# Shared expert moved into the routed expert loop, bodies of 18 tiles, gates applied as rows leave PSUM

## The reference, cut to what matters

```python
x = x + tanh(g_xattn) * xattn(layernorm(x), ctx_768)      # 16 heads, 77 keys
flat = layernorm(x)                                       # 8192 tokens x 128
scores = softmax(flat @ router_w.T + router_bias)         # 32 experts
topk_scores, topk_idx = top_k(scores, 4)                  # normalised to sum 1
h = silu(flat @ gate_w[e].T) * (flat @ up_w[e].T)         # per chosen expert e, H = 128
out = sum_k topk_scores[k] * (h @ down_w[e_k].T)
out = out + silu(flat @ sgate_w.T) * (flat @ sup_w.T) @ sdown_w.T   # shared expert, 512 wide
x = x + tanh(g_ffn) * out
```

## Time and profile before

| | |
|---|---|
| runs | 1175.61, 1176.28, 1176.44 us, median 1176.28 |
| profiled execution | span 1462.0 us; no other time of it is given |
| attention and routing, to about 760 us of the trace | 760 us |
| table and two shared chunks, 760 to 804 us | 44 us |
| expert loop, 804 to 1304 us | 500 us |
| tail, 1304 to 1462 us | 158 us |
| busy over the span | PE 79%, DVE 54%, ACT 51%, POOL 46% |

### The profile page before, as it was taken

How to read it: one execution, slowest core, us unless ns; L and a number is a source line. 1 busy time by engine, 2 the same in 40 slices (tenths; PEclk the granted TensorE clock), 3 DMA queues, 4 the chain that set the end, 5 groups by cost and what they waited for, 6 DMA issues and landing times.

```text
span 1462.0 us, 27745 instructions
## 1 busy us (share of the span) xinstructions
PE 1161.1 (79%) x6592; PEld 874.1 (60%) x6593; DVE 784.3 (54%) x3017; ACT 746.2 (51%) x2533; POOL 673.6 (46%) x947
## 2 busy tenths in 40 slices
PE   5888988888888888888876776676767766779997
PEld 3666766666766766666753555454555555545664
DVE  4766666666665666666652333333333333338777
ACT  4776766776766776766741433343333333322221
POOL 1355555454545454555563555555555555540000
PEclk9988889898898989989978888888878788889999
DMA  6200000000000000001212222222222222225443
GB/s 179 92 25 24 26 28 27 24 24 24 28 25 27 25 24 24 24 28 29 102 41 70 76 79 72 77 77 71 72 70 74 74 73 76 70 65 154 133 120 109
DMA packets 90282, 89.96 MB, mean 62 GB/s; under 512 B 21293, under 2 KB 71578, under 8 KB 89876
## 3 DMA queue, kind: packets, MB, share of 16 engines
q1 hardware_dynamic: 72468, 55.17, 13.7%
q0 software_dynamic: 17792, 34.53, 7.0%
HBM read 49.57 MB, written 42.16 MB: 63 GB/s over the span
## 4 chain that ended last, share of the span: by engine, by line
PE 55%; issue 13%; another core or an unknown queue 12%; ACT 12%; DVE 4%; DMA 2%; POOL 1%; ACTq 0%; SPq 0%; POOLq 0%; DVEq 0%
PE ps L1067 9%; PE ps L976 7%; PE ps L1032 6%; PE ps L936 6%; ACT qT L510 5%; PE ps L1078 4%; PE ps L1041 3%; PE ps L1073 3%; PE ps L941 2%; PE ps L1062 2%; PE ps L1015 2%; PE ps L1018 2%; PE ps L913 2%; ACT sg L571 1%
## 5 line engine op out<-in xcount | busy, mean ns | idle before, releaser
L432 POOL DMA_INDIRECT y_rows<-y_sb,didx x288 | 283.0, 983 | 236.0 <-DVE y_sb L839 140.7
L414 POOL DMA_INDIRECT x_rows<-payload,slot x256 | 251.3, 982 | 220.9 <-DVE slot L754 158.5
L1067 PE MATMUL ps<-w_gu,xT 128*128 x576 | 211.4, 454 | 70.4 <-issue 68.6
L571 ACT ACTIVATE sg<-ps 128x128 f32<-128x128 f32 x288 | 80.9, 281 | 269.4 <-PE ps L1067 120.1
L828 DVE TENSOR_TENSOR h<-sg,ps 128x128 f32<-128x128 f32 x288 | 82.9, 288 | 206.2 <-ACT sg L571 113.6
L976 PE MATMUL ps<-kvbd,qT 128*128 128x308 f32 x512 | 191.4, 484 | 0.0
L936 PE MATMUL ps<-vt,pT 128*128 128x108 f32 x1024 | 162.4, 309 | 0.0
L936 PEld LDWEIGHTS ps<-vt,pT 128*128 128x128 f32 x1024 | 145.0, 219 | 14.1 <-issue 9.2
L1067 PEld LDWEIGHTS ps<-w_gu,xT 128*128 128x128 f32 x576 | 105.3, 228 | 79.7 <-issue 79.5
L1073 PE MATMUL ps<-cst,h 128*128 128x128 f32 x288 | 96.9, 337 | 68.2 <-issue 38.6
L839 DVE COPY y_sb<-ps 128x128 f32<-128x128 f32 x288 | 82.7, 287 | 120.9 <-remote 81.6
(11 more groups left out here) (130 smaller groups left out, 2288.2 us busy)
## 6 DMA issues: line engine op xcount, KB each, us to landing
xin<-x_rows SPq DMA_DIRECT2D x288, 64.5 KB
w_gu<-y_rows SPq DMA_DIRECT2D x16, 1024.0 KB, 5.7
y_rows<-y_sb,didx POOLq DMA_INDIRECT x288
w_gu<-in_gu SPq DMA_DIRECT2D x2, 2048.0 KB, 10.1
x_rows<-payload,slot POOLq DMA_INDIRECT x256
out<-w_gu SPq DMA_DIRECT2D x16, 256.0 KB, 2.5
w_dn<-in_dn SPq DMA_DIRECT2D x1, 2048.0 KB, 9.2
ctx_sb<-in_ctxT SPq DMA_DIRECT2D x64, 29.2 KB
```

Source lines behind the costliest of these rows:

```text
L414: nc.gpsimd.indirect_dma_start(x_rows, bass.IndirectOffsetOnAxis(ap=slot[:, v, k:k + 1], axis=0), payload[:, v, k, :], None).then_inc(sent ...
L432: nc.gpsimd.indirect_dma_start(y_rows, bass.IndirectOffsetOnAxis(ap=didx[:, u:u + 1], axis=0), y_sb[:, u, :], None, bounds_check=TOKENS * ...
L1067: nc.tensor.matmul(bank[2 + u % 2][:, 0:2 * H], xT[:, u % 2, :], w_gu[:, bass.ds(e * (2 * H), 2 * H)], start=True, stop=True).then_inc(gu_ ...
```

## The change

1. The expert loop runs 16 bodies of `U3` = 18 tiles. `xin` and `y_sb` have 18 slots each. At the head of a body PE reads 20 numbers and SP 18.
2. The first 12 bodies (`MID`) each hold one chunk of the shared expert, a unit from each of the tiles 0, 4, 9 and 13 (`UNIT_AT`): its gate matmul in that tile, its up matmul one tile later, its product on DVE two later, its down matmuls three later. The tail keeps chunks 14 and 15.
3. The shared expert needs three PSUM banks in the loop, so three of the four results of a tile have one bank (`ps_xT`, `ps_hT`, `ps_dn`). `turn_x` now waits for the copy of the turn before, `down` for the copy of the result before (`y_d`), and PE's order within a tile is `gate_up`, `down`, `turn_h`, `turn_x`.
4. A row of `x_rows` carries its gate as a 130th column. `result` multiplies by it where it only copied. `take_dest` and `didx` are gone: POOL takes the row numbers from `xin`, so a slot of `xin` is free only when its scatter has landed.
5. The tail sums in place: four additions of 512 columns a chunk on `x_all`, from four slots of loaded rows; the stores read `x_all`.

```diff
-U3 = 8
+U3 = 18
+PER = 2
+UNIT_AT = (0, 4, 9, 13)
+MID = 12
...
+        ps_xT, ps_gu, ps_hT, ps_dn, ps_g, ps_u, ps_y = bank[0], bank[1:3], bank[3], bank[4], bank[5], bank[6], bank[7]
...
+        def bodies(eng, body):
+
+            body(0, shared=True, first=True)
+            with eng.Fori(1, MID) as j:
+                body(j, shared=True)
+            with eng.Fori(MID, TG - 1) as j:
+                body(j, shared=False)
+            body(TG - 1, shared=False, last=True)
...
                 for u in range(U3):
 
-                    tile_done(sp, didx_d, n, u)
+                    need(sp, y_sent[u], 16 * j)
                     sp.dma_start(xin[:, u, :], x_rows[bass.ds(firsts[u], 128), :]).then_inc(xin_in[u], 16)
...
-                nc.vector.tensor_copy(didx[:, u:u + 1], xin[:, u, D:ROW].bitcast(U32)).then_inc(didx_d[u % 4], 1)
...
-                nc.vector.tensor_copy(y_sb[:, u % U3, :], bank[6 + u % 2][:, 0:D]).then_inc(y_d[u % 4], 1)
+                nc.vector.tensor_scalar(y_sb[:, u % U3, :], ps_dn[:, 0:D], xin[:, u % U3, D + 1:ROW], None,
+                                        ALU.mult).then_inc(y_d[u % PER], 1)
...
+            def body(j, shared, first=False, last=False):
+                n = counts(dve, j, U3 // PER)
                 for u in range(U3):
                     hidden(n, u)
                     if not (first and u < 2):
                         result(n, u - 2)
+                    if shared and u - 2 in UNIT_AT:
+                        mixed_hidden(j, UNIT_AT.index(u - 2))
+                if shared:
+                    mixed_take(j)
...
+                for k in range(TOPK):
+                    if k:
+                        dve.wait_ge(acc_d, TOPK * c + k)
+                    nc.vector.tensor_tensor(xs, xs, yld[:, c % 4, :, k, :], ALU.add).then_inc(acc_d, 1)
...
                 for u in range(U3):
                     gate_up(n, u, es[u + 2])
+                    if shared and u in UNIT_AT:
+                        mixed_gate(j, UNIT_AT.index(u))
+                    if shared and u - 1 in UNIT_AT:
+                        mixed_up(j, UNIT_AT.index(u - 1))
+                    if shared and u - 3 in UNIT_AT:
+                        mixed_down(j, UNIT_AT.index(u - 3))
+                    if not (first and u < 2):
+                        down(n, u - 2, es[u])
                     if not (first and u == 0):
                         turn_h(n, u - 1)
                     if not (last and u >= U3 - 2):
-                        turn_x(n16, u + 2)
-                    if not (first and u < 2):
-                        down(n, u - 2, es[u])
+                        turn_x(n16, n, u + 2)
```

More of the change, by code:

```diff
@@ L36 @@
 EARLY = 2
-ROW = D + 1
+MID = 12
+ROW = D + 2
 STRIDE = TOKENS + 128
@@ L90, in build @@
         x2T = sb("x2T", [128, T])
-        gates = sb("gates", [128, B * TOPK])
         tg = sb("tg", [128, 2])
@@ L585, in body @@
                         evac(n, u + 2)
+                    if shared and u in UNIT_AT:
+                        mixed_silu(j, UNIT_AT.index(u))
             for u in range(2):
                 evac(counts(act, 0, 1), u)
[L589 to L596, removed]
+            bodies(act, body)
+            h_turned(counts(act, TG - 1, U3 // PER), U3 - 1)
+            with act.Fori(EARLY + MID, CHUNKS) as j:
                 for u in range(4):
@@ L843, in body, with mixed_take @@
+            def mixed_take(j):
+                c = EARLY + j
+                xs = x_all[:, bass.ds(c * 4 * D, 4 * D)]
+                need(dve, sy_p, 16 * c + 16)
+                nc.vector.scalar_tensor_tensor(out=xs, in0=ps_y[:, :], scalar=tg[:, 1:2], in1=xs,
+                                               op0=ALU.mult, op1=ALU.add).then_inc(take_d, 4)
+            def body(j, shared, first=False, last=False):
+                n = counts(dve, j, U3 // PER)
                 for u in range(U3):
@@ L886, in _ @@
-            with dve.Fori(1, CHUNKS // 2 - 1) as j:
-                chunk(2 * j + 1, 1)
-                chunk(2 * j + 2, 0)
-            chunk(CHUNKS - 1, 1)
+                combine(c - late)
             take(CHUNKS - 1)
-            for k in range(TOPK):
-                combine(CHUNKS - 1, 1, k)
+            for c in range(CHUNKS - late, CHUNKS):
+                combine(c)
         @block.tensor
@@ L1081, in tiles, with units, mixed_gate @@
-            def tiles(j, first=False, last=False):
+                tile_done(pe, y_d, n, u - 1)
+                after(nc.tensor.matmul(ps_dn[:, 0:D], hT[:, u % 2, :], w_dn[:, bass.ds(e * D, D)], start=True,
+                                       stop=True), hT_d, n, u).then_inc(dn_p[u % PER], 1)
+            def units(j, k):
+                unit = 4 * (EARLY + j) + k
+                return unit if isinstance(unit, int) else pe.to_reg(unit)
+            def mixed_gate(j, k):
+                unit = units(j, k)
+                nc.tensor.matmul(ps_g[:, :], w[:, W_SG + 128 * k:W_SG + 128 * (k + 1)],
+                                 x2T_all[:, bass.ds((EARLY + j) * 512, 512)], start=True,
+                                 stop=True)._wait_ge(ssg_d, unit).then_inc(sg_p, 1)
@@ new lines, in mixed_up, with mixed_down @@
+            def mixed_up(j, k):
+                unit = units(j, k)
+                nc.tensor.matmul(ps_u[:, :], w[:, W_SU + 128 * k:W_SU + 128 * (k + 1)],
+                                 x2T_all[:, bass.ds((EARLY + j) * 512, 512)], start=True,
+                                 stop=True)._wait_ge(hs_d, unit).then_inc(sg_p, 1)
+            def mixed_down(j, k):
+                unit = 4 * (EARLY + j) + k
+                need(pe, hs_d, unit + 1)
+                if k == 0:
+                    need(pe, take_d, unit)
+                for q in range(4):
+                    nc.tensor.matmul(ps_y[:, q * D:(q + 1) * D], hs[:, k % 2, q * 128:(q + 1) * 128],
+                                     w[:, W_SD + 128 * k:W_SD + 128 * (k + 1)], start=k == 0 and q == 0,
+                                     stop=k == NS - 1 and q == 3).then_inc(sy_p, 1)
@@ L1083, in tiles, with body @@
+            def body(j, shared, first=False, last=False):
                 es = numbers(pe, tab_sb, j * TW + U3, U3 + 2, E - 1)
-                n, n16 = counts(pe, j, U3 // 4), counts(pe, j, 2, dma=True)
+                n, n16 = counts(pe, j, U3 // PER + 1), counts(pe, j, 2, dma=True)
                 for u in range(U3):
                     gate_up(n, u, es[u + 2])
+                    if shared and u in UNIT_AT:
+                        mixed_gate(j, UNIT_AT.index(u))
[5 more added lines that the diff above has]
+                        down(n, u - 2, es[u])
```

181 lines of the change are left out of this document (81 added, 100 removed).

## The result

The changed kernel takes 1244.96 us (median of 4 runs, 1244.07 to 1246.05), the one before 1176.13 us beside it: a ratio of 1.058, interval 1.057 to 1.060. The forecast was +17 us; the runs gave +69. Its sign holds, its size does not.

The account below looks back on a forecast made before the run. POOL was taken to bound the old loop and plain bodies, PE the bodies with a chunk. Tail -74, loop +90 and tables +1 gave +17 us, 1193 us against 1176, with a range of 1132 to 1218.

Parts of the forecast that it names:

- The budget of before: Time of the kernel before by stage: tail 158 us, 64 attention steps 552, start, drain and table about 70, loop 388.
- unexplained stretches: Pieces in the loop and attention of the first profile that no instruction explains, such as 3.41 us, read as profiling cost.
- POOL as the bound of the old loop: A scatter every 1.29 us on POOL against 0.87 us a tile on PE; PE idles 0.42 us a tile.
- The tail: Tail after the change, with 8 units and 16 chunks of sums: 78 to 95 us, taken as 84, saving 74 us.
- Wait one: In bodies with a chunk, `mixed_down` in tile u+3 waits 0.79 us for `hs` from DVE, 3.2 us in four units.
- Wait two: With one PSUM bank, `down` waits for the previous tile's `result`: mostly covered beside chunks, plain tiles 0.87 to about 1.05 us.
- Wait three, the boundary: PE's pause between bodies, with 20 numbers to load: bounded by 1.6 and 3.1 us, taken as 2.1 us.
- The falling clock: Rival, chance 0.12: first two tiles behind each boundary at half clock, 1.7 us lost twelve times, +20 us, 1213 us.
- the 31.4 us forecast: Length of a loop body with a chunk: 26.1 us of PE work, 3.2 for `hs`, 2.1 for the boundary; twelve times 377.

Follow-up runs that it names:

- aligned run: Changed kernel with table rows padded to 160 bytes, so that both groups of numbers start on a multiple of 16 bytes: 1214.61 us, ratio 1.033.
- the one with every body off: Changed kernel with rows of 160 bytes but PE's numbers 8 bytes past a multiple of 16 in every body: 1272.37 us, ratio 1.085.
- eight chunks spread: Changed kernel, table aligned, last projection one tile later, two units in each of 16 bodies at tiles 4 and 13: 1133.6 us, ratio 0.967.

## Why the forecast was wrong in size

**The budget of before** (tail 158, loop 388, unexplained stretches not real) was right within 5 us, and POOL as the bound of the old loop too.

**The tail** took 70 us, forecast 84. The additions were as bounded, 0.69 us each:

```profile
L895 DVE TENSOR_TENSOR x_all<-x_all,w_gu x64: 680/692/694, 1182.2 to 1240.7; 128x512 f32<-128x512 f32 x64
```

What was off is the rate: 300 GB/s at a share of 0.86, where the earlier trace rows had 253 at 0.81. The Trainium skill's 425 GB/s for a large load ("DMA: Bandwidth & Descriptors", Bandwidth) would have put it, by an estimate, at some 65 us. Over the whole tail this case shows 300, nearer the row than the page, and the time of 70 us lies nearer the estimate's.

**Wait one** (0.79 us at `hs`) was right: 0.70 us in the rows above, and in the run with the projection a tile later it is gone.

**Wait two** was right for plain tiles: PE's own time for a plain body with a short load is 21.8 us in the aligned runs, forecast 21. In bodies with a chunk I counted it as covered by shared matmuls "in most tiles", and put the others at nothing. With the projection a tile later, 29.35 us less 1.5 for the pause leave 27.9 us where 26.1 were forecast. The trace of the aligned kernel with the later projection shows where they are, in two following tiles without a shared matmul:

```profile
846.54 0.60 PE L1084 MATMUL ps<-w_gu,xT 128*128 x2
847.55 0.60 PE L1084 MATMUL ps<-w_gu,xT 128*128 x2
847.64 0.27 ACT L592 COPY hT<-ps 128x128 f32<-128x128 f32 x1 [0.19 <-PE ps L1089]
847.68 0.34 DVE L856 TENSOR_SCALAR y_sb<-ps,xin 128x128 f32<-128x128 f32 x1
848.17 0.48 PE L1095 MATMUL ps<-w_dn,hT 128*128 x2
848.71 0.60 PE L1084 MATMUL ps<-w_gu,xT 128*128 x2
```

The tiles take 1.01 and 1.16 us from start to start, and those with a shared matmul 0.87 and the matmul (1.73 us). In the second tile `down` (L1095) could start 0.43 us behind `gate_up`, at 847.98. It starts 0.15 us behind the end of `y_sb` at 848.02, the copy out of its one result bank; `hT` had ended at 847.91. In the first tile the two end within 0.02 us of each other. That is wait two. Eight of the 18 tiles are such tiles: 4 x (1.01 + 1.16 - 2 x 0.87) = 1.7 of the 1.8 us. A second result buffer was not tried; by these rows it would not remove all of it, since `hT` comes only a little earlier.

**Wait three, the boundary, is the step that failed.** "I bound the boundary by 1.6 (length does not matter) and 3.1 us (twice) and take 2.1." I took min 1.07 and median 1.84 of the earlier trace rows as a spread around one price. They are two prices, by the start address, and the one boundary of the earlier trace rows was a short one. With 20 numbers the long price is 4.9 us, the pause 5.8. The aligned run puts this at 30 us, the one with every body off at another 27.

**The falling clock**, a rival at 0.12 and +20 us, held beside it, and the sum had it at nothing. I had argued that a pause of 1.57 us stood at clock 1.00. That row covers the pause alone, but the body behind it had no half clock either, and such pauses keep the clock in all profiles but that stretched first one. Those of the changed kernel are 2.3 and 5.8 us. The Trainium skill ("TensorE: Matmul & The Clock Gate", HAM oscillation) tells of a loop that waits some 3 to 5 us for a transfer in each pass and starts each pass cold. The forecast stretched that to its own pause of 2 us, which the page does not state. Here every body with a chunk of the changed kernel had half clock, behind 2.0 to 5.8 us, and none behind 1.5 us in the later versions.

A price of 1.7 us for 12 bodies is 20 us. It holds for the longer bodies too, though they have 6.8 us at half clock. The pause before a longer body, and what follows it, kernel after:

```profile
778.13:783.65 5.52, 0.00 (x0) 0.00 (x1) 0.97 (x3) 0.36 (x2) 1.97 (x2) 0.69 0.23 61
783.65:787.10 3.45, 3.45 (x8) 2.24 (x9) 0.34 (x2) 0.28 (x1) 0.00 (x0) 0.50 0.08 19
```

The clock fell while PE stood: (1 - 0.69) x 5.52 / 0.5 = 3.4 of the 6.8 us lie in the pause and cost nothing. The other 3.4 us lie on work, as in the short bodies.

The changed kernel's own shorter bodies have 1.3 us over: 34.2 less 26.1, 4 x 0.70 of `hs`, 2.35 of pause and 1.7 of clock. Five of their six tiles without a shared matmul take 1.01 us, 0.14 more than counted; most of the rest is 0.1 us in each tile of a last projection (2.57 us for 0.87 + 0.89 + 0.70).

The account, with each body's parts against the 31.4 us forecast: +17 forecast, +30 for the long loads, 12 x 1.7 = +20 for the clock, 12 x (1.3 + 0.25 - 0.4) = +14 for wait two, the pause and the cheaper `hs`, +5 because the loop before was shorter, +1 at the start, -14 in the tail. That is +73 where +69 were measured.

**Why the idea pays little even when repaired.** In spans: with the table aligned, no chunk in the loop 1169.5 us; eight chunks spread, 1131.4. Scatters from first to last went from 370.0 to 392.5 us, +22.5; the tail from 158.3 to 97.0, -61.3. In four-unit bodies the loop pays 6.1 us for a chunk that gives 7.3 back, in spread ones 22.5 / 8 = 2.8 us, since the first 1.4 us of each body lie under POOL.

## What to carry to other kernels

A loop that reads numbers into registers at each pass pays by where they start: look at the single loads, not at min and median, and pad the table's rows so that each load starts on a multiple of 16 bytes. Here that gave 2.4% where PE bound the loop and 0.6% where POOL did. Put the load where matmuls are still queued, so that part of it is hidden and the pause stays short enough for the clock. And before work is moved from one stage to another, find what it costs at both ends by its slope (us per chunk), since a stage's shortest time seen is not a floor under which more work is free.

## What the runs showed of the hardware

- A load of 20 numbers into PE's registers took 1.4 to 1.55 us from a multiple of 16 bytes, 4.9 to 5.3 us from 8 bytes past one; 10 numbers some 1.15 and 2.5 us. SyncE's 18 numbers took 1.4 to 1.6 us, and 3.7 to 3.9 us in the changed kernel where they start 8 bytes past, which is the other half of the bodies.
- In all profiles but the stretched first one: behind pauses of PE of up to 1.76 us no time at half clock followed in the bodies behind the first; in the kernel before with its table aligned, where all pauses are 1.4 to 1.75 us, none of the looped bodies had any. Behind pauses of 2.0 to 2.5 us either none or 3.4 us did, in the same kernel, and once 6.8; behind some 3 us in the kernel before mostly 3.4 us; behind 5 us and more 6.8 us, in single cases 10.2. Of 6.8 us at a pause of 5.8 us, 3.4 lay in the pause itself and cost nothing; 3.4 us on work cost 1.7.
- A profiled execution can be 24% longer than the timed ones (1462 against 1176 us) and another of the same kernel agree with them (1175.1). The stretches without an explanation were the sign.
